# Second-half gathers that add into x by themselves, in an attention and mixture-of-experts block

## The reference

```
xn  = layernorm(x)
# attention: 16 heads of 8 features, plus a context term common to all heads
ctx = xn @ We.T;  influence = ctx @ ctx.T
attn = softmax(Q @ K.T / sqrt(8) + 0.1 * influence)
a    = concat(attn @ V) @ Wo.T
# experts: each token goes to the two best of 8
probs = softmax(xn @ gate_w.T);  top 2
y = sum over the 2 choices of  prob * (gelu(xn @ w1[e] + b1[e]) @ w2[e] + b2[e])
out = x + a + y
```

## Time and profile before

| | |
|---|---|
| time, median of 3 runs | 715.39 us (713.87 to 716.93) |
| span of the profiled execution | 791.5 us |
| PE busy | 671.2 us (85%) |
| DVE busy | 619.4 us (78%) |
| ACT busy | 538.9 us (68%) |
| POOL busy | 467.2 us (59%) |
| DMA queues of SP, of POOL | 46.2% and 8.6% of 16 engines |

### The profile page before, as it was taken

One profiled execution on the slowest core, in us unless ns is written; L12 is line 12 of the kernel. 1 busy time (PEld: TensorE's weight loads), 2 busy tenths in 40 slices (PEclk: granted clock), 3 DMA queues, 4 the chain that ended last, 5 costly groups with the idle time before them and its releaser, 6 DMA issues.

```text
span 791.5 us, 24553 instructions
## 1 busy us (share of the span) xinstructions
PE 671.2 (85%) x7800; PEld 433.1 (55%) x7800; DVE 619.4 (78%) x1106; ACT 538.9 (68%) x1123; POOL 467.2 (59%) x542
## 2 busy tenths in 40 slices
PE   0477888989889896969999999996689989988886
PEld 0463344444444443559999999993244444444444
DVE  8989878878778785948888888885587888887871
ACT  2581566776667685858888888884466766766765
POOL 8650656666566555306555565656676676676671
PEclk9997899999999998999999999999699999999998
DMA  9779545665455653664555454443376666566632
GB/s 262 253 212 299 138 125 146 154 175 158 117 159 148 176 155 100 174 111 90 101 105 102 96 109 102 103 89 100 77 153 161 159 165 166 152 161 161 159 92 61
DMA packets 162947, 113.32 MB, mean 143 GB/s; under 512 B 72624, under 2 KB 150448, under 8 KB 162864
## 3 DMA queue, kind: packets, MB, share of 16 engines
q1 hardware_dynamic: 153632, 90.63, 46.2%
q0 software_dynamic: 8192, 16.86, 8.6%
q10 hardware_dynamic: 1040, 4.76, 1.6%
HBM read 55.42 MB, written 47.19 MB: 130 GB/s over the span
## 4 chain that ended last, share of the span: by engine, by line
PE 71%; DVE 7%; issue 7%; SPq 5%; ACT 4%; another core or an unknown queue 3%; DMA 1%; ACTq 0%; DVEq 0%
PE bank L1133 20%; PE bank L1111 13%; PE bank L1251 12%; PE mx L1240 12%; PE mx L1145 7%; ACT A L708 4%; DVE mx L956 2%; PE bank L1193 2%; PE bank L1031 2%; PE bank L1162 2%; DVE A L791 2%; PE bank L1155 1%; SPq L319 1%; SPq L318 1%
## 5 line engine op out<-in xcount | busy, mean ns | idle before, releaser
L708 ACT ACTIVATE A<-bank 128x512 f32<-128x512 f32 x502 | 279.1, 602 | 109.9 <-PE bank L1133 94.1
L956 DVE TENSOR_REDUCE mx<-mx 128x4 f16<-128x1024 f32 x256 | 303.7, 1208 | 56.3 <-PE mx L1145 26.8
L1133 PE MATMUL bank<-stack 113*128 113x256 f16 x1004 | 185.2, 283 | 51.2 <-issue 24.9
L565 POOL DMA_INDIRECT slots_x<-rows,pos x128 | 123.5, 965 | 91.3 <-PE bank L1133 68.0
L579 POOL TENSOR_SCALAR rows<-rows,slot_p 128x128 f32<-128x128 f32 x142 | 112.1, 798 | 103.4 <-DVE rows L1007 103.4
L609 POOL DMA_INDIRECT rows<-slots_y,pos x128 | 121.5, 950 | 73.4 <-PE bank L1133 54.6
L1133 PEld LDWEIGHTS bank<-stack 113*128 113x128 f16 x1004 | 66.9, 99 | 164.9 <-issue 85.7
L1111 PE MATMUL bank<-A,V 128*32 128x256 f32 x2048 | 142.2, 397 | 1.7 <-ACT A L708 1.6
L752 ACT ACTIVATE rows<-mx,b 128x256 f32<-128x256 f32 x284 | 111.8, 474 | 30.0 <-PE mx L1240 30.0
L1001 DVE TENSOR_TENSOR rows<-rows 128x512 f16<-128x512 f32 x142 | 101.2, 714 | 25.2 <-ACT rows L756 22.8
L1251 PE MATMUL bank<-w,rows 128*128 x1704 | 108.2, 220 | 4.4 <-DVE rows L1001 4.4
(11 more groups left out here) (142 smaller groups left out, 616.8 us busy)
## 6 DMA issues: line engine op xcount, KB each, us to landing
stack<-ctx_rest SPq DMA_DIRECT2D x64, 256.0 KB
stack<-qk_dram SPq DMA_DIRECT2D x128, 96.0 KB
slots_y<-rows SPq DMA_DIRECT2D x71, 128.0 KB, 2.0
qk_dram<-hi_qk SPq DMA_DIRECT2D x64, 128.0 KB
stack<-ctx_high SPq DMA_DIRECT2D x128, 64.0 KB
slots_x<-A ACTq DMA_DIRECT2D x1, 4644.0 KB, 20.2
w_stage<-in_w SPq DMA_DIRECT2D x8, 512.0 KB
qk_dram<-lo_qk SPq DMA_DIRECT2D x64, 64.0 KB
```

The source lines that it names most:

```text
L565: pool.indirect_dma_start(slots_x, bass.IndirectOffsetOnAxis(pos[j][:, t:t + 1], 0), rows[:, t, :].bitcast(F32), None).then_inc(s_scat, 16)
L708: act.activation(A[:, n % NA, :, :].rearrange("p h s -> p (h s)"), scores(k, n)[:, :], ACT.Exp, scale=SCALE).then_inc(s_xp, 1)
L956: dve.tensor_reduce(mx[:, a, 8 * qt:8 * qt + 8].rearrange("q (i e w) -> q i e w", i=2, e=2)[:, :, g % 2], MX[u % 2][:, :].rearrange("q (i ...
L1133: mm = pe.matmul(scores(k, n)[:, i * S:(i + 1) * S], stack[0:SHIFT + 1, par, h, 1, c * P:(c + 1) * P], stack[0:SHIFT + 1, par, h, 0, :], s ...
```

## The change

The scratch buffer `ye2`, both additions and the semaphores `s_both` and `s_sum` go. Each gather now reads its 128 rows from `slots_y` and adds them to the tile in `x` in the transfer itself (`compute_op=ALU.add`). The second choice of a tile (`m` 4 to 7) waits until the first choice of the same tile has landed. Gathers with even `m` wait for ScalarE's exponentials (`s_xp`) instead of TensorE's products, and those with odd `m` for one shifted product fewer than before. The waits on `s_sum` become waits on the landed second choices: VectorE for `m` 6 and 7 (second-half tiles) before L970, SyncE for `m` 4 and 5 (first-half tiles) before the stores. Inside the loop their thresholds are worked out from its register.

```diff
-        ye2 = [free[:, 16 * D * i:16 * D * (i + 1)].bitcast(F32).rearrange("p (m d) -> p m d", m=8) for i in range(2)]
...
-        s_yp, s_both, s_sum = sem("s_yp"), sem("s_both"), sem("s_sum")
+        s_yp = sem("s_yp")
...
                     sp.wait_ge(s_acc, b + 1 if isinstance(b, int) else sp.to_reg(b + 1))
+                    for m in (4, 5):
+                        sp.wait_ge(s_yg[s.r][m], 16 * (s.half - 1 - HALF // 2) + 16)
...
-            halves = x[:, :, :].rearrange("p (h t) d -> p h t d", h=2)
-            def add_choices(n):
-                for m in range(8):
-                    pool.wait_ge(s_yg[n % 2][m], 16 * (n // 2) + 16)
-                pool.tensor_tensor(ye2[n % 2][:, 0:4, :], ye2[n % 2][:, 0:4, :], ye2[n % 2][:, 4:8, :], ALU.add).then_inc(s_both, 1)
-            def add_experts(n):
-                pool.wait_ge(s_both, n + 1)
-                pair = halves[:, :, 2 * n:2 * n + 2, :]
-                pool.tensor_tensor(pair, pair, ye2[n % 2][:, 0:4, :].rearrange("p (h t) d -> p h t d", h=2), ALU.add).then_inc(s_sum, 1)
             for n in range(HALF):
                 for m in range(8):
                     j, i = m // 4, m % 4
                     t = 2 * n + i if i < 2 else 2 * (n + HALF) + i - 2
-                    pool.wait_ge(s_ex, 16 * (HALF + n) + 2 * (m - LEAD) + 2)
-                    if n >= 2:
-                        pool.wait_ge(s_sum, n - 1)
-                    pool.indirect_dma_start(ye2[n % 2][:, m, :], None, slots_y, bass.IndirectOffsetOnAxis(pos[j][:, t:t + 1], 0)).then_inc(s_yg[n % 2][m], 16)
-                    if m == 3 and n:
-                        add_choices(n - 1)
-                    if m == 5 and n:
-                        add_experts(n - 1)
-            add_choices(HALF - 1)
-            add_experts(HALF - 1)
+                    if m % 2:
+                        pool.wait_ge(s_ex, 16 * (HALF + n) + 2 * (m - LEAD) + 1)
+                    else:
+                        pool.wait_ge(s_xp, 16 * (HALF + n) + 2 * (m - LEAD))
+                    if j == 1:
+                        pool.wait_ge(s_yg[n % 2][m - 4], 16 * (n // 2) + 16)
+                    pool.indirect_dma_start(x[:, t, :], None, slots_y, bass.IndirectOffsetOnAxis(pos[j][:, t:t + 1], 0), compute_op=ALU.add).then_inc(s_yg[n % 2][m], 16)
...
                         if not first_half:
-                            dve.wait_ge(s_sum, bc - HALF + 1)
+                            for m in (6, 7):
+                                dve.wait_ge(s_yg[s.r][m], 16 * (s.half - 1 - HALF // 2) + 16)
```

## The result

The changed kernel takes 748.08 us (median of 4 runs, 745.92 to 748.49), the kernel before 716.16 us in the same comparison: ratio 1.0443, 95% interval 1.0417 to 1.0469. It is 32 us slower. I had forecast no change (715.4, range 705 to 723).

What follows compares the result with a forecast made beforehand. The prediction took TensorE to bound the second attention stage. Its terms, 0 for the additions, 0 for the gathers and 0 for the waits, left the median at 715.4 us, range 705 to 723.

Steps and rivals of the forecast that it cites:

- The bound of the stage: Second attention stage: TensorE busy 91% of 14.73 us steps, GpSimd 69%; no engine but TensorE near full.
- How early GpSimd is: GpSimd's last addition against the L970 that needs it: 8.9 us spare at the smallest, some 18 us in the loop.
- The additions: GpSimd's L594 and L600, 40.9 us or 2.56 us per step, not on the chain: gain 0 from removing them.
- The gathers: GpSimd's issue of 128 accumulating gathers, taken at 1.0 us each, hidden up to 1.58 us: cost 0.
- The transfers: Gathers' DMA work taken as twice as much, step share 0.66 to 0.83; SyncE's loads keep 4.7 us spare: cost 0.
- B: Theory of the experiments, not the prediction: the accumulation fills the DMA engines and transfers land late.
- The waits: New waits on GpSimd, VectorE before L970 and SyncE before stores, and the earlier releases: all hidden, cost 0.
- Slower by the gather's issue: Rival, chance 0.07: GpSimd's issue costs 1.90 us per gather, L970 waits 41 us for the last, 752 us.
- The faster rival: Chance 0.30: spread-out gathers remove half of TensorE's 11.1 us stall in the opening, 5.0 us of the median: 710.4.
- The DMA engines: Rival, chance 0.06: accumulating gathers take four times the engine time, share 1.17, 27 us of the median: 742.
- VectorE's new waits: Rival, chance 0.09: uncovered waits before L970 cost 0.24 us per step and delay TensorE as much: 721.9.
- The signs of being wrong: L970 or L1145 waits for a transfer, gathers back to back, other step length, or opening stall changed over 3 us.

Runs made afterwards that it cites:

- The doses of memset: Changed kernel with plain gathers, no expert result added, and a GpSimd memset of 400, 560 or 760 float32 behind each: 715.20, 726.08 and 748.71 us.
- the second profile: The kernel before, unchanged, profiled again: 714.74 us, span 713.0.
- 560: Changed kernel with plain gathers, no expert result added, and a GpSimd memset of 560 float32 behind each: 726.08 us, ratio 1.0179.

## Why the prediction was wrong, point by point

**The bound of the stage.** That TensorE holds the stage of the kernel before and GpSimd is not on the chain was right. How near GpSimd was to it was wrong: "GpSimd for 50.74 (69%)" and "some 12.9" of "14.73" came from a disturbed execution. Undisturbed it is 12.4 of 13.2 us.

**How early GpSimd is.** "8.9 us are spare where the slack is smallest" and "In the loop it is larger" were readings of the disturbed execution too. Undisturbed the smallest slack is that of the first sequence, 2.0 us, and at the end it is 7.1.

**The additions.** Worth 0, right: shown by the plain gathers at 715.22 us.

**The gathers: the step that failed.** "0 for the gathers" measured 31.9 us. Two things went into it, and neither alone would have given the zero away. First the value: "I take 1.0", measured 1.548, inside my bounds of 0.95 and 1.90 but far from the end that I took. The nearest row was no guide, as the trace had no accumulation. Second, the price that would matter: "1.89 us per gather, so 1.58 us of issue with the gap", by which 1.548 would still have been hidden. I had worked it out as (788.3 - 542.2 - 4.3) / 128, deadlines of the disturbed execution. From the undisturbed one the same sum is (709.78 - 502.66 - 3.4) / 127 = 1.60 (128 gathers have 127 steps between them), less 0.30 for the gap 1.30 us. The doses of memset bear it out: 1.58 us with the gap is hidden, 1.71 is not. A price of 1.0 would have been hidden under this threshold as well, and that of 1.548 is not. I had seen the 76 us between span and median, and scaled the result by 0.904, but not the deadlines. Yet that scaling alone shows the danger: 14.73 x 0.904 = 13.3 us a step, and 1.89 x 0.904 = 1.71 us per gather with its gap, 1.41 of issue, while GpSimd's instructions keep their durations, as the second profile shows.

**The transfers.** "I take twice": measured 29.5% of 242.1 us for 128 gathers, 0.558 us each, against 18.4% of 213 us, 0.306, in the undisturbed run of before, 1.8 times. The Trainium skill, "Collectives: The Full Stack", section "The bandwidth ceiling: the fold count and why AG ≠ RS ≠ AR", has a reduction with two source reads at about half the rate of a copy; at 1.8 times this case's trace agrees. That the second read is the cause is not shown: at half of the width a gather still takes 0.39 us (49.6 / 128), so part of it does not go with the bytes. That the added load costs nothing was right as far as the runs show: all of the loss comes back with the memsets at half of the changed kernel's share, and a third less load at half of the width changes nothing clear of noise. What is left of B is small: a landing of 3.4 us in place of 2.6 (737.54 to 740.92, against 718.43 to 721.00 with 560), paid once, at the end.

**The waits.** 0, right: GpSimd never rests long enough for the wait for a first choice to show, the releases alone change nothing (0.9999), and the run with plain gathers has all the new waits, VectorE's and SyncE's too, at 715.22 us.

**The rivals.** "Slower by the gather's issue" is what happened; I gave it 0.07 and worked out 752 us for an issue of 1.90 us; at 1.548 it is 748.08. The mechanism was right and the nearness of the two numbers is luck: the price was 0.35 us too high and the threshold 0.28 us too high. With the undisturbed terms an issue of 1.90 us would give a span of 502.18 + 127 x 2.20 + 3.4 + 3.2 = 788 us, an estimate. With 1.853 in place of 2.20 the terms make 744.1, the measured span, from whose trace they are taken. Its chance was too small because the threshold looked comfortable. The faster rival rested on the stall of TensorE in the earlier trace rows, and that stall belonged to the disturbed execution: from the first gather to the first L970 it took 39.2 us there and takes 21.9 undisturbed (502.66 to 524.54). The DMA engines and VectorE's new waits did no harm that the runs show beyond that landing.

**The signs of being wrong.** L970 came to wait for a transfer, and the gathers stand back to back. Only the first tells the two kernels apart: back to back they stand in the undisturbed kernel before as well. The step of 14.7 us that I forecast is there too (14.71 above), but it is paced by GpSimd, and that it is as long as the disturbed one is a coincidence; the undisturbed kernel before has 13.2.

What disturbed the first profiled execution is open; no run was made on it. The two traces of the kernel before say where it sat. The first L1133 starts at 81.4 us in the one and at 80.8 in the other; and the expert stage, from the first to the last start of L1251, takes 188.1 us (349.0 to 537.1) and 188.8 (308.8 to 497.6). So nearly all of the extra time lies in the two attention stages.

## What to carry to other kernels

Before anything is read from a profile, hold its span against the timed runs. Where they differed by a tenth here, single durations were still right, but deadlines, gaps and shares were not, and each "how much is spare" must be redone with steps of the timed length. An engine off the chain has a capacity all the same: here 13.2 us a step, of which 12.4 were used, and eight gathers without additions could have cost 1.60 us each with the gap, 0.35 more than plain ones, but not 1.85. Trading an engine's arithmetic for a dearer form of its own DMA issue pays only if the sum per step goes down, and where the engine is off the chain even then it gains nothing.

## What the runs showed of the hardware

- An accumulating indirect gather of 128 rows of 512 bytes costs GpSimd 1.548 us, a plain one 0.952, with 0.30 us to the next in both cases.
- It is cut up differently: 18432 packets for 128 gathers, 144 each, against 4096, 32 each. With 64 rows it is 10240, 80 each, so one for each row and 16 more.
- The transfers of one such gather keep all 16 DMA engines busy for 0.558 us, those of a plain one for 0.306; with 256 bytes per row it is 0.39.
- Half of the bytes per row leaves the issue at 1.548 us, half of the rows makes it 1.419.
- Two profiled executions of one kernel had spans of 791.5 and 713.0 us, with the same durations of single GpSimd instructions (gather 950 and 952 ns) and steps of 14.73 and 13.2 us.
